# Wider count buffers, later sign rows and paired source one-hots in a graph convolution kernel

## The reference

```python
def gcn_conv(x, W, b, src, dst, n):
    h = x @ W
    deg = jnp.zeros((n,), h.dtype).at[dst].add(1.0) + 1.0
    dinv = jax.lax.rsqrt(deg)
    norm = dinv[src] * dinv[dst]
    agg = jax.ops.segment_sum(h[src] * norm[:, None], dst, num_segments=n)
    return agg + h * (dinv * dinv)[:, None] + b

src, dst = (edge_index[0], edge_index[1])
h = gcn_conv(emb, W1, b1, src, dst, NTOKEN)      # 64 -> 128
nodes = gcn_conv(h, W2, b2, src, dst, NTOKEN)    # 128 -> 64
return nodes[input.reshape(-1)].reshape(b_, l_, NINP)
```

## Time and profile before

| | us |
|---|---|
| median of 3 runs | 2952.67 (2952.14 to 2952.69) |
| the profiled execution, its own time | 2957.68 |
| its span | 2955.9 |

### The profile page before, as it was taken

The page is one execution under the profiler, slowest core; times in us unless marked ns, Lnnn a source line. Parts: engine busy times, 40 slices in busy tenths (PEclk is TensorE's granted clock), DMA queues, the critical chain, the costliest instruction groups (busy, mean ns, idle before and its releaser), DMA issues.

```text
span 2955.9 us, 93772 instructions
## 1 busy us (share of the span) xinstructions
PE 2166.1 (73%) x36894; PEld 1793.7 (61%) x36895; DVE 2672.2 (90%) x8846; ACT 1913.9 (65%) x5195; POOL 736.2 (25%) x704
## 2 busy tenths in 40 slices
PE   2455555555561777777788888895999999999980
PEld 2445544444321666666677666674888888888870
DVE  9999999999987888888999999995999999999970
ACT  5878778878663764545466656664777776777760
POOL 2000000000000222222623333310313234545546
PEclk9556566665685888999899999997999999999995
DMA  4000000000023333333345555556667775555631
GB/s 105 1 1 1 1 1 1 1 1 1 22 64 42 109 96 92 93 99 93 78 100 115 123 122 121 119 129 183 163 208 208 212 205 157 139 140 141 141 101 20
DMA packets 226744, 276.99 MB, mean 94 GB/s; under 512 B 109050, under 2 KB 121834, under 8 KB 226044
## 3 DMA queue, kind: packets, MB, share of 16 engines
q1 hardware_dynamic: 203996, 243.55, 28.7%
q0 software_dynamic: 22304, 27.40, 6.9%
HBM read 219.15 MB, written 51.81 MB: 92 GB/s over the span
## 4 chain that ended last, share of the span: by engine, by line
DVE 45%; PE 44%; issue 5%; ACT 2%; POOL 2%; DMA 1%; SPq 1%; another core or an unknown queue 1%; DVEq 0%; POOLq 0%
PE ps L1318 23%; PE ps L1266 14%; DVE oh L1882 11%; DVE keys L1558 7%; DVE keys L1559 6%; DVE oh L1410 6%; PE ps L1202 3%; DVE keys L1808 2%; DVE keys L1576 1%; DVE keys L1577 1%; DVE arena L1410 1%; PE ps L1292 1%; DVE keys L1601 1%; DVE k_e L1650 1%; POOL out L868 1%
## 5 line engine op out<-in xcount | busy, mean ns | idle before, releaser
L1084 ACT ACTIVATE grow_t<-ps 128x384 bf16<-128x384 f32 x2744 | 1148.0, 497 | 706.7 <-PE ps L1266 636.0
L1882 DVE TENSOR_SCALAR oh<-io_h,dl 128x256 bf16<-128x256 int16 x5476 | 1167.2, 294 | 32.2 <-remote 15.2
L1318 PE MATMUL ps<-grow_t,oh 128*128 128x192 bf16 x10952 | 1083.8, 251 | 7.6 <-issue 5.5
L1318 PEld LDWEIGHTS ps<-grow_t,oh 128*128 128x128 bf16 x10952 | 900.3, 100 | 140.2 <-issue 118.0
L1266 PE MATMUL ps<-arena,keys 128*32 128x192 bf16 x21952 | 622.1, 252 | 191.6 <-DVE keys L1808 99.2
L1266 PEld LDWEIGHTS ps<-arena,keys 128*32 128x32 bf16 x21952 | 448.0, 98 | 325.9 <-issue 288.6
L995 ACT ACTIVATE grow_t<-colf,arena 128x128 bf16<-128x128 f32 x1888 | 555.2, 391 | 33.5 <-PE ps L1130 33.5
L907 POOL DMA_INDIRECT zring<-table,sidx x296 | 298.9, 1010 | 706.5 <-PE ps L1266 668.8
L1130 PE MATMUL ps<-oh,grow_t 128*128 128x147 bf16 x1888 | 244.0, 302 | 237.6 <-ACT grow_t L995 172.5
L1130 PEld LDWEIGHTS ps<-oh,grow_t 128*128 128x128 bf16 x1888 | 194.0, 129 | 283.4 <-issue 152.1
L1808 DVE TENSOR_SCALAR keys<-keys,rowf 128x1024 bf16<-128x1024 int16 x686 | 336.3, 490 | 25.1 <-DMA keys<-srel 7.6
(11 more groups left out here) (232 smaller groups left out, 1452.0 us busy)
## 6 DMA issues: line engine op xcount, KB each, us to landing
keys<-srel SPq DMA_DIRECT2D x686, 256.0 KB
out<-res SPq DMA_DIRECT2D x50, 512.0 KB
table<-arena SPq DMA_DIRECT2D x19, 384.0 KB, 2.8
table<-sgn_l SPq DMA_DIRECT2D x73, 96.0 KB
zring<-table,sidx POOLq DMA_INDIRECT x296
nodes<-arena SPq DMA_DIRECT2D x73, 64.0 KB
arena<-in_L_rec_edge_index SPq DMA_DIRECT2D x2, 1171.5 KB, 6.0
arena<-nodes,oidx POOLq DMA_INDIRECT x108
```

The source lines that it names most:

```text
L1084: act.activation(grow[:, (layer * NB + j) % DEEP, h * 2 * ROW:(h + 1) * 2 * ROW], psum[HALF_BANK[layer][HB * j + h][0]][:, 0:2 * ROW], ACT ...
L1318: mm = pe.matmul(sums(sl, k), dwin[:, (layer * NB + j) % DEEP, t, k * P:(k + 1) * P], grow[:, (layer * NB + j) % DEEP, t * ROW:(t + 1) * ROW],
L1882: made = dve.tensor_scalar(dwin[:, (layer * NB + j) % DEEP, c % BT, :], io_h[:, :], dl[:, c:c + 1], None, ALU.is_equal)
```

## The change

The count gets eight block buffers for five and eight step buffers for four; the new ones lie in memory that is unused in this stage. DVE makes every sixth half's lane one-hot, not every fifth (49 for 58; ACT 245 for 236). One step in six gets a third block one-hot, and a turn gets none: `PER_STEP` is (2, 2, 2, 2, 2, 3) and `PER_TURN` 0. ACT makes lanes up to `BUILT[n] + 3` before a turn. The lists change as follows: the last half is built in step 149, not 151, and the turn at which the count ends stays the same one.

The iotas of the sign rows wait for the fifth block one-hot, not the first. That fifth one stands behind the operations that make the keys (L1482 to L1490). DVE's own part of the sign rows moves from there to step 16.

In the layers, a source one-hot is made for two batches at once: NP = 172 operations of 128 x 2048 instead of 343 of 128 x 1024, in every second iteration, with three buffers of `s_oh` and two of `srow`, each twice as large. The loads are as large as two before.

```diff
-LANES_BY_DVE = [n for n in range(HALVES) if n % 5 == 4]
-LANES_BY_ACT = [n for n in range(HALVES) if n % 5 != 4]
-BLOCK_BUFS, LANE_BUFS, STEP_BUFS = 5, 2, 4
-AT_ONCE, PER_STEP, PER_TURN = 8, (2,), 1
+LANES_BY_DVE = [n for n in range(HALVES) if n % 6 == 5]
+LANES_BY_ACT = [n for n in range(HALVES) if n % 6 != 5]
+BLOCK_BUFS, LANE_BUFS, STEP_BUFS = 8, 2, 8
+AT_ONCE, PER_STEP, PER_TURN, AHEAD_OF_TURN = 8, (2, 2, 2, 2, 2, 3), 0, 3
...
-SBUFS = 4
+SBUFS = 3
+RBUFS = 2
+PT = 2 * BT
+NP = -(-NB // 2)
...
             def sources_in(layer, p):
-                sp.wait_ge(s_ready, layer * NB + max(p - SBUFS + 1, 0) + FREE)
+                sp.wait_ge(s_ready, layer * NP + max(p - RBUFS + 1, 0) + FREE)
                 if layer == 0:
-                    sp.wait_ge(rel_out, 16 * (p * BT // P + 1))
-                n = min(BT, GT * P - p * BT)
-                sp.dma_start(srow[:, p % SBUFS, 0:n * P],
-                             srel[p * BT:p * BT + n, :].rearrange("t e -> (t e)").rearrange("(a x) -> a x", a=1)
-                             .to_broadcast([P, n * P])).then_inc(srow_in[p % SBUFS], 16)
+                    sp.wait_ge(rel_out, 16 * (p * PT // P + 1))
+                sp.dma_start(srow[:, p % RBUFS, :],
+                             srel[p * PT:(p + 1) * PT, :].rearrange("t e -> (t e)").rearrange("(a x) -> a x", a=1)
+                             .to_broadcast([P, PT * P])).then_inc(srow_in[p % RBUFS], 16)
...
-                    if layer == 0 or p >= SBUFS:
-                        sources_in(layer, p)
+                    if p % 2 == 0 and (layer == 0 or p // 2 >= RBUFS):
+                        sources_in(layer, p // 2)
...
-            pool.wait_ge(hist_oh, 1)
+            pool.wait_ge(hist_oh, AT_ONCE // 2 + 1)
             pool.iota(sgn_t[:, 6, :], pattern=[[0, P]], base=0, channel_multiplier=0,
...
             def lanes_before(n):
-                return HALVES if n >= LAST_TURN else BUILT[n] - 1
+                return HALVES if n >= LAST_TURN else min(BUILT[n] + AHEAD_OF_TURN, HALVES)
...
-                pe.wait_ge(s_ready, layer * NB + FREE + 1)
+                pe.wait_ge(s_ready, layer * NP + FREE + 1)
 
                 def gather_half(x):
                     bank_free(*HALF_BANK[layer][x][1])
-                    if x and x % HB == 0:
-                        pe.wait_ge(s_ready, layer * NB + FREE + x // HB + 1)
+                    if x and x % (2 * HB) == 0:
+                        pe.wait_ge(s_ready, layer * NP + FREE + x // (2 * HB) + 1)
...
-            dve.wait_ge(iotas, 4 + SB - 6)
-            link(dve.tensor_scalar(sgn_t[:, 6, :], sgn_t[:, 6, :], odd[:, 0:1], None, ALU.add))
-            for sgn in (sgn_t[:, 6:7, :], sgn_l):
-                link(dve.tensor_scalar(sgn[:, :, :], sgn[:, :, :], 1.0, -2.0, ALU.is_equal, ALU.mult))
-                link(dve.tensor_scalar(sgn[:, :, :], sgn[:, :, :], 1.0, None, ALU.add))
             for n in range(AT_ONCE // 2, AT_ONCE):
                 one_hots(n)
+
+            def signs():
+                dve.wait_ge(iotas, 4 + SB - 6)
+                link(dve.tensor_scalar(sgn_t[:, 6, :], sgn_t[:, 6, :], odd[:, 0:1], None, ALU.add))
+                for sgn in (sgn_t[:, 6:7, :], sgn_l):
+                    link(dve.tensor_scalar(sgn[:, :, :], sgn[:, :, :], 1.0, -2.0, ALU.is_equal, ALU.mult))
+                    link(dve.tensor_scalar(sgn[:, :, :], sgn[:, :, :], 1.0, None, ALU.add))
...
                 deg_step(i - DEG_AT)
+                if i == 16:
+                    signs()
...
                 def s_build(p):
-                    dve.wait_ge(srow_in[p % SBUFS], 16 * (layer * len(range(p % SBUFS, NB, SBUFS)) + p // SBUFS + 1))
+                    dve.wait_ge(srow_in[p % RBUFS], 16 * (layer * len(range(p % RBUFS, NP, RBUFS)) + p // RBUFS + 1))
                     if p >= SBUFS:
-                        dve.wait_ge(gmm, HB * layer * NB + HB * (p - SBUFS + 1))
-                    dve.tensor_scalar(s_oh[:, p % SBUFS, :], srow[:, p % SBUFS, :], rowf[:, 0:1], None, ALU.is_equal).then_inc(s_ready, 1)
+                        dve.wait_ge(gmm, HB * layer * NB + 2 * HB * (p - SBUFS + 1))
+                    dve.tensor_scalar(s_oh[:, p % SBUFS, :], srow[:, p % RBUFS, :], rowf[:, 0:1], None, ALU.is_equal).then_inc(s_ready, 1)
...
-                    if j + 1 < NB:
-                        s_build(j + 1)
+                    if j % 2 == 0 and j // 2 + 1 < NP:
+                        s_build(j // 2 + 1)
```

More of the change, by code:

```diff
@@ L174, in gcn_program @@
         keys_h = keys[:, :].bitcast(BF16)
-        s_oh = keys_h[:, 0:SBUFS * BT * P].rearrange("p (s e) -> p s e", s=SBUFS)
-        srow = keys_h[:, SBUFS * BT * P:2 * SBUFS * BT * P].bitcast(I16).rearrange("p (s e) -> p s e", s=SBUFS)
+        s_oh = keys_h[:, 0:SBUFS * PT * P].rearrange("p (s e) -> p s e", s=SBUFS)
+        srow = keys_h[:, SBUFS * PT * P:(SBUFS + RBUFS) * PT * P].bitcast(I16).rearrange("p (s e) -> p s e", s=RBUFS)
         k_e = sb("k_e", [P, COLS], F32)
@@ L186, in gcn_program @@
         iorep = sb("iorep", [P, BLOCKS, TT], BF16)
[L187 to L190, removed]
+        oh = sb("oh", [P, max(5 * BLOCKS * HH, DEEP * BT * SUP * P)], BF16)
+        grow_t = sb("grow_t", [P, max(4 * P * HH, DEEP * BT * ROW)], BF16)
+        steps_oh = [grow_t[:, n * P * HH:(n + 1) * P * HH] for n in range(4)]
+        block_oh = [oh[:, n * BLOCKS * HH:(n + 1) * BLOCKS * HH] for n in range(5)]
         LANES_AT = 4 * EC + LANE_BUFS * P * HH // 2
@@ L194, in gcn_program @@
         key_t = raw[:, LANES_AT:LANES_AT + ECOLS]
+        MORE_AT = LANES_AT + EC
+        more_blocks = raw[:, MORE_AT:MORE_AT + 3 * BLOCKS * HH // 2].bitcast(BF16)
+        block_oh += [more_blocks[:, n * BLOCKS * HH:(n + 1) * BLOCKS * HH] for n in range(3)]
         grow = grow_t[:, 0:DEEP * BT * ROW].rearrange("p (s e) -> p s e", s=DEEP)
@@ L198, in gcn_program @@
         ooh = sb("ooh", [P, OHRING, SUP * P], BF16)
+        for spare in (zring, ooh):
+            flat_spare = spare[:, :, :].rearrange("p n e -> p (n e)")
+            steps_oh += [flat_spare[:, n * P * HH:(n + 1) * P * HH] for n in range(2)]
         res = sb("res", [P, 2, BB * F], F32)
@@ L331, in gcn_program @@
         mini_out = sem("mini_out")
-        srow_in = [sem(f"srow_in{s}") for s in range(SBUFS)]
+        srow_in = [sem(f"srow_in{s}") for s in range(RBUFS)]
         s_ready = sem("s_ready")
@@ L774, in _ @@
                 if layer == 0:
-                    for p in range(SBUFS):
+                    for p in range(RBUFS):
                         sources_in(1, p)
@@ L994, in lanes @@
                         for t in range(HH):
-                            last_step = act.activation(steps_oh[:, s % STEP_BUFS, t * P:(t + 1) * P], colf[:, :], ACT.Sign,
+                            last_step = act.activation(steps_oh[s % STEP_BUFS][:, t * P:(t + 1) * P], colf[:, :], ACT.Sign,
                                                        bias=nlo[:, n * HH + t:n * HH + t + 1])
@@ L1117, in count_half @@
             def count_half(n):
-                blk = block_oh[:, n % BLOCK_BUFS, :].rearrange("p (s j t) -> p s j t", s=HH // TT, t=TT)
+                blk = block_oh[n % BLOCK_BUFS].rearrange("p (s j t) -> p s j t", s=HH // TT, t=TT)
                 pe.wait_ge(hist_oh, n + 1)
@@ L1125, in count_half @@
                     s = LANES_BY_ACT.index(n)
-                    stp = steps_oh[:, s % STEP_BUFS, :].rearrange("p (t j) -> p t j", j=P)
+                    stp = steps_oh[s % STEP_BUFS].rearrange("p (t j) -> p t j", j=P)
                     pe.wait_ge(hist_steps, s + 1)
@@ L1266, in gather @@
                         mm = pe.matmul(bank[q * ROOM:(q + 1) * ROOM, t % 2 * ROW:(t % 2 + 1) * ROW],
-                                       s_oh[:, j % SBUFS, t * P + q * ROOM:t * P + (q + 1) * ROOM],
+                                       s_oh[:, j // 2 % SBUFS, (j % 2 * BT + t) * P + q * ROOM:(j % 2 * BT + t) * P + (q + 1) * ROOM],
                                        xtab[:, (w * WIN + q) * ROW:(w * WIN + q + 1) * ROW], start=True, stop=True)
@@ L1417, in one_hots @@
                     dve.wait_ge(hist_mm, n - BLOCK_BUFS + 1)
-                compared(block_oh[:, n % BLOCK_BUFS, :], dhi, BLOCKS, n).then_inc(hist_oh, 1)
+                compared(block_oh[n % BLOCK_BUFS], dhi, BLOCKS, n).then_inc(hist_oh, 1)
                 if n in LANES_BY_DVE:
@@ L1913, in _ @@
                             dve.wait_ge(tab1_out[n], 16 * TAB1[n])
-                        for p in range(SBUFS):
-                            dve.wait_ge(srow_in[p], 16 * (len(range(p, NB, SBUFS)) + 1))
+                        for p in range(RBUFS):
+                            dve.wait_ge(srow_in[p], 16 * (len(range(p, NP, RBUFS)) + 1))
                     else:
```

## The result

| | before | after |
|---|---|---|
| median, us | 2952.68 (4 runs, 2952.14 to 2952.72) | 2866.56 (4 runs, 2863.90 to 2873.28) |
| profiled execution, us | 2957.68 | 2865.14 |
| its span, us | 2955.9 | 2863.3 |

The changed kernel takes 0.9712 of the time (95% interval 0.9695 to 0.973): 86.1 us less by the medians, 92.6 by the two spans. In the changed kernel L1410 is L1418, L1482 to L1485 are L1490 to L1493, L1558 is L1568, L1577 is L1589, L805 is L813, L995 is L1003, L1048 is L1056, L1266 is L1274, L1318 is L1326, L1739 is L1751, L1808 is L1820 and L1882 is L1894.

What follows compares the result with a forecast made beforehand. DVE bounds the sort and later layer 0, no engine early layer 0, PE layer 1. Sort 41.4, layer 0 47 and layer 1 0, together 88 us off the median 2952.7, give 2864 us; range 2838 to 2898.

Steps and rivals of the forecast that it cites:

- Sign rows: Start of the sort: two DVE key operations collide with POOL's iotas; moving the iotas later takes 12.0 us off.
- rival that iotas disturb exchanges: Sort: moved iotas slow the two-way exchanges beside them, losing the 12 us again, 2876 us; chance 0.08.
- Turn waits: Sort: 18 waits of DVE's block one-hots for PE, 25.0 us, go; less 1.0 for ACT, 24.0 us gained.
- nine lane one-hots: Sort and count: DVE makes 49 for 58, at 0.60 us each, 5.4 us gained; ACT gets 21 us more work.
- wait for ACT at turn 3: Sort, turn 3: ACT's copies come 2.4 us late against 1.2 us to spare, so DVE waits 1.2 us.
- Width of the pair: Layer 0: one 2048-wide source comparison takes 0.66 us where two take 0.80; 172 pairs give 24 us.
- Looser coupling: Layer 0: PE no longer waits for source one-hots behind prepare, fewer slow gathers follow; 20 us, bounds 5 and 30.
- layer 0 keeps its period: Rival, layer 0: the 17.07 us period stays, so 20 and 8 us are lost, 2892 us; chance 0.20.
- The list: Layer 0: SP reaches the list of surplus units earlier, so 4 of the 7.9 us that DVE waits are gained.
- First source wait: Before the first source comparison: the load is twice as large, so DVE's 3.73 us wait grows by about 1 us.
- Layer 1: Second layer: the pairs' gain is hidden behind PE, 0 us; a change of more than 5 us would be wrong.
- Late sources: Rival, layer 1: with two source buffers, 10 us loads make each pair 0.8 us late, 3002 us; chance 0.05.

Runs made afterwards that it cites:

- E5: The changed kernel itself, run once more beside the kernel before on one of the later chips: 2831.24 us against 2905.70 (0.9749).

## Why the prediction was right, and where it wasn't

2864 was forecast and 2866.56 came out. The mechanisms of the sort and of the width were right, and they carry some 65 of the 88 us. That the sum came so near is partly luck: the idle time of layer 0's first part fell short of its term by 7 us and the list by 4, while layer 1 gave 5, the sort 2.6 and the rest of layer 0 some 8 more than forecast. One term held in part where it was made and nowhere else, and one did not come.

- **Sign rows, 12.0.** Right in place and size: 1.37 and 1.38 us, iotas done at 50.0, 11.0 us by themselves. The rival that iotas disturb exchanges fell: the first four take 1.29 to 1.34 us beside them, and 1.34 to 1.36 without them in the kernel before. So the two tensor_scalar operations were held up beside the iotas, 3.72 and 11.01 us for 1.37 and 1.38, and the tensor_tensor operations there were not. What makes the difference no run shows.
- **Turn waits, 24.0, and nine lane one-hots, 5.4.** Right together: the sort came out 44.0 us shorter (ACT's first ranking operation, after the sort, starts at 895.6 for 939.6) where 41.4 was forecast, and 30.2 against 29.4 in the experiment. The wait for ACT at turn 3 was forecast at 1.2 us and is 0.89. No loss to ACT stands against them: DVE's waits for ACT's copies came to 13.0 us before and 11.9 after, where 1.0 more was forecast. Eight buffers alone gave 27.6, the 25.0 and the overlaps that the waits had cost. The lane one-hots are 5.2 us of DVE's busy time between the kernels with eight buffers alone and with the count's whole part, 5.4 by the forecast; 0.8 of it comes back as idle time, so the sort is 4.3 shorter.
- **Width of the pair, 24.** Right: the step from start to start is 0.66 us as forecast, and the experiment gives 24 us.
- **Looser coupling, 20.** Of the right sign on the first machine, too large there, and zero on the later chips with the same code. DVE's idle time in the first part of layer 0 fell by 13 us (58 to 45) instead of by 20, the period to 16.2 instead of 15.5 to 16, and DVE's waits for PE to some 23 us instead of 10. The step that failed is the reading of the earlier trace rows as something that the order makes (PE idles in `prepare`, then gathers slowly). PE idles there as well in the kernel with the sign rows alone, 2.2 us before the gather, and the slow gathers do not follow. On the first machine the change took away PE's waits for the source comparison (24.6 us to none in the stretches above), and the gaps stayed, 39.7 of 48.4 us. The number of slow gathers went from 18 to 10 there, in one trace of each kernel; whether through the order, the load pattern or chance no run could tell. What makes them stays open. The rival "layer 0 keeps its period" asked the right question; the misses of this term and of layer 1 lie on opposite sides and nearly cancel.
- **The list, 4.** Wrong: 7.95 us is left of 7.93. DVE did come 9.98 us after the write's issue and not 6.3, so the 3.7 us were there; but the write took 7.6 us to the read for 5.0, and the read 10.3 to DVE's start for 9.2, which ate them. SP's transfers, first before and then after:

```profile
1353.03 1.09 SPq L719 DMA_DIRECT2D over<-arena  x1
1358.03 0.24 SPq L721 DMA_DIRECT2D arena<-over  x1
```

```profile
1283.91 0.44 SPq L728 DMA_DIRECT2D over<-arena  x1
1291.49 0.25 SPq L730 DMA_DIRECT2D arena<-over  x1
```

  The write's time goes with the loads and not with the chip: it lands in 5.0 to 5.2 us in all five traces with 256 KB loads, in 7.5 to 7.8 in all eight with 512 KB loads and two buffers, and in 5.6 with 512 KB loads and one buffer, where a load waits until the one before it has been compared. That points to the larger loads already on their way when it is issued; why the read takes longer was not taken apart. The experiment with the later rounds shows the other half: this wait hid another, since SP stands behind the write.
- **First source wait, 1.** Right: 4.80 for 3.73 us.
- **Layer 1, 0.** 5.1 us came. On the later chips layer 1 takes 808 to 812 us with pairs or without (but for the single source buffer), and on the first machine it took 820.4 and then 815.3: what it gained there it gained from an excess whose cause is open. I had set 5 us as the mark for being wrong here, and it stands on the mark.
- **Late sources (3002).** It didn't come. No run made the loads themselves slow; with one buffer less, late sources cost some 100 us, so the case was worth its place.

The layers' terms together were to give 47 us. The table of cuts has 22.5 + 7.2 + 15.0 - 1.1 = 43.6 in layer 0 (the 1.1 is the longer first wait, which lies ahead of the first cut) and 5.1 in layer 1: 48.7. With 44.0 of the sort, less 0.2 at the end, that is the 92.6 of the spans, within rounding; the medians, 86.1 apart, differ by less because the profiled execution of the kernel before lies 5.0 us above its median and that of the changed one 1.4 below. Of layer 0's 43.6, 24 are the width and 13 the idle time; the rest is of the size of the 6.2 us that two narrow operations gained in pairs, but that it is the same was not shown.

## What to carry to other kernels

Before a stall is charged to the order of the work, look whether its picture is the same in a trace from another chip: here 20 of the 47 us forecast for the layers hung on stalls that none of the later chips has. When a wait is taken from an engine, follow the queue of the one that it waited for: SP's stand behind one write showed first as DVE waiting for a list, and, when that was put off, as DVE waiting for sources. And try an added resource alone: three more block buffers gave 27.6 of the 30.2 us that the changed constants of the count gave together.

## What the runs showed of the hardware

- The same kernel took 2952.7 us on the first machine and 2905.7 to 2907.5 on the later chips. By the traces, of which the first machine's lies 5 us above its median, 40 us of difference are in layer 0 up to the list (402.8 against 362.4 us with the sign rows alone) and 10 in layer 1 (820.4 against 810.0). What makes the gather's weight loads start some 0.7 us apart on the one (at 1259.31, 1260.03, 1260.73 and 1261.45 us) is open. The profile names nothing that they wait for, and no run could turn it on. Longer transfers are not seen: from 967 to 1300 us a DMA packet of the hardware queue took 0.082 us in the mean there, and 0.084 in the kernel with the sign rows alone on chip 12.
- A DVE comparison of 2048 columns costs 0.663 us from start to start and one of 1024 costs 0.396 (medians, where DVE is full). So 1024 more columns cost 0.267 us, and by that slope 0.13 us (an estimate, 0.396 less 0.267) belong to the operation and not to its columns.
- A write of 352 KB landed in 5.0 to 5.2 us among loads of 256 KB and in 7.5 to 7.8 among loads of 512 KB, also on one and the same chip, and in 5.6 where those loads could not be under way two at a time.
- The granted clock in the first part of layer 0 was 0.90 and 0.92 on the first machine, and on the later chips 0.94 with the order of before, 0.98 with batches built one further ahead and 1.00 in E5, while that part's length on the later chips was 362.4 and 361.4 us in the first two of these: there the clock moved, and the time hardly did.
